# Two heads of 16 dimensions in two row tiles: scores and maxima of the narrow attention, in steps of two key chunks

## The reference

```python
# x: normalized queries; keys, values: the context
q, k, v = split_heads(x @ Wq), split_heads(ctx @ Wk), split_heads(ctx @ Wv)   # 16 heads of 16
scores = einsum('bhqd,bhkd->bhqk', q, k) / sqrt(16)
scores = where(arange(4096) < valid_lens[b], scores, -1000000.0)
out = einsum('bhqk,bhkd->bhqd', softmax(scores), v) @ Wo
```

## Time and profile before

| | us |
|---|---|
| median of 3 runs | 4371.15 (4368.67 to 4373.83) |
| the profiled execution: its own time | 4371.64 |
| its span, from first to last instruction | 4369.9 |
| narrow attention's cycles, 2732 to 3775 | 1043 |
| in the whole span: TensorE busy | 3948.9 (90%) |
| VectorE busy | 2704.8 (62%) |
| ScalarE busy | 2369.3 (54%) |

### The profile page before, as it was taken

How to read it: one execution, slowest core, us unless ns; L and a number is a source line. 1 busy time by engine, 2 the same in 40 slices (tenths; PEclk the granted TensorE clock), 3 DMA queues, 4 the chain that set the end, 5 groups by cost and what they waited for, 6 DMA issues and landing times. The chain is left out here.

```text
span 4369.9 us, 74948 instructions
## 1 busy us (share of the span) xinstructions
PE 3948.9 (90%) x26760; PEld 2746.4 (63%) x26760; DVE 2704.8 (62%) x4112; ACT 2369.3 (54%) x4373; POOL 1552.2 (36%) x1229
## 2 busy tenths in 40 slices
PE   5899999999999999998677976999999999676599
PEld 2677777777777777776446965555555555343365
DVE  4766666666666666663264124677776777476666
ACT  2677777777777777776142112555555566444111
POOL 1566666666666666666022003000000000033000
PEclk9999999999999999999788987999999999888799
DMA  5777767777677666662203647544444422100011
GB/s 194 273 252 252 248 241 260 256 256 250 239 265 252 247 232 222 232 224 80 78 10 121 266 171 261 151 156 137 142 148 141 120 58 65 31 2 5 18 37 42
DMA packets 232703, 724.77 MB, mean 166 GB/s; under 512 B 44557, under 2 KB 129805, under 8 KB 163725
## 3 DMA queue, kind: packets, MB, share of 16 engines
q1 hardware_dynamic: 229664, 711.78, 47.8%
q0 software_dynamic: 2688, 8.39, 0.5%
HBM read 625.70 MB, written 94.37 MB: 165 GB/s over the span
## 5 line engine op out<-in xcount | busy, mean ns | idle before, releaser
L752 POOL TENSOR_TENSOR wa_acc<-wa_acc,wa_probs 128x512 f32<-128x512 f32 x960 | 1246.5, 1298 | 525.1 <-ACT wa_probs L613 444.9
L677 DVE TENSOR_REDUCE wa_mx<-wa_ps_m 128x2 f32<-128x1024 f32 x512 | 626.6, 1224 | 486.1 <-PE wa_ps_m L488 485.9
L613 ACT ACTIVATE wa_probs<-wa_ps_s 128x512 f32<-128x512 f32 x1024 | 556.3, 595 | 525.5 <-PE wa_ps_s L534 520.2
L1204 ACT ACTIVATE na_probs<-na_ps_s 128x512 f32<-128x512 f32 x1024 | 564.1, 599 | 377.8 <-PE na_ps_s L1108 372.4
L1256 DVE TENSOR_REDUCE na_mx<-na_ps_m 128x1 f32<-128x512 f32 x1024 | 643.0, 681 | 186.8 <-PE na_ps_m L1093 185.8
L605 ACT ACTIVATE wa_ps_s<-wa_m_wide 128x512 f32<-128x512 f32 x1024 | 575.7, 605 | 1.0
L510 PE MATMUL wa_ps_o<-wa_probs,wa_values 128*64 128x256 f32 x4096 | 505.3, 389 | 0.0
L1093 PE MATMUL na_ps_m<-na_keys,na_q 98*128 98x512 f32 x1024 | 425.8, 424 | 41.7 <-DVE na_mx L1256 28.6
L1108 PE MATMUL na_ps_s<-na_q,na_keys 100*128 100x512 f32 x1024 | 429.8, 427 | 2.4 <-ACT na_probs L1204 1.6
L449 PE MATMUL wa_ps_k<-wa_k_ctx,wa_w_k 128*128 128x512 f32 x1488 | 388.6, 396 | 0.0
L475 PE MATMUL wa_ps_v<-wa_w_v,wa_v_ctx 128*128 128x256 f32 x2880 | 382.5, 282 | 0.0
(11 more groups left out here) (329 smaller groups left out, 5108.6 us busy)
## 6 DMA issues: line engine op xcount, KB each, us to landing
wa_k_ctx<-ctx_split SPq DMA_DIRECT2D x248, 1024.0 KB, 5.1
wa_v_ctx<-ctx_split SPq DMA_DIRECT2D x120, 1024.0 KB, 5.7
na_ctx<-ctx_split SPq DMA_DIRECT2D x56, 1024.0 KB, 6.9
na_keys<-k_rows SPq DMA_DIRECT2D x192, 256.0 KB
ctx_split<-wa_stage SPq DMA_DIRECT2D x32, 1024.0 KB, 9.7
wa_land<-in_ctxT SPq DMA_DIRECT2D x32, 512.0 KB, 10.3
ge_w_b<-in_w_rows SPq DMA_DIRECT2D x8, 2048.0 KB
k_rows<-na_k_high SPq DMA_DIRECT2D x64, 256.0 KB, 2.3
```

The lines of the kernel that those rows point to most:

```text
L613: act.activation(probs[:, c % R:c % R + 2, h * SQ:(h + 1) * SQ], ps_s[n % BANKS][:, :].rearrange("p (c n) -> p c n", c=2), ACT.Exp).then_i ...
L677: dve.tensor_reduce(mx[:, half, :, k], ps_m[:, :, :], AX.X, ALU.max).then_inc(m_taken, 1)
L752: pool.tensor_tensor(acc[:, :], acc[:, :], probs[:, c % R, :], ALU.add).then_inc(summed, 1)
L1204: act.activation(probs[:, n % RP, :], ps_s[n % RS][:, :], ACT.Exp).then_inc(exp_done, 1)
```

## The change

Each head of the pair gets a row tile of its own: its four mask and shift rows and 48 key rows lie at rows 0 to 51 for the first head and 64 to 115 for the second. `q` loses the second block and its zeros.

- Scores come in steps (`t`, 16 a cycle) of two chunks: four products of 52 rows x 256 columns, two for each head. A bank of `ps_s` now holds one head's scores for two chunks. There are still three banks, and a step begins when the exponentials of all but the last bank are done (n+2-3).
- Maxima come in units (`u`, 16 a cycle): the same 128 queries of both heads, two products of 52 rows x 512 columns into two banks. The rows of the shift, which the maxima must not see, are cleared by GpSimd (`clear_shift`, two small instructions a cycle).
- The order of a cycle's work changes: the last weighting of a cycle goes into the next cycle's step 1, `turn_maximum` goes ahead of the second half of the values' projection, `copy_out` from the cycle's start to step 2, `divide` to step 4. The shift is copied by two instructions.
- The keys of one half are loaded by 8 transfers, where there were 4.

```diff
     DH = 16
     W = 2 * DH
-    MASK = 3 * W
-    MROWS, ROWS = MASK + 2, MASK + 4
+    HEAD = 64
+    KEYS = 4
+    ROWS = KEYS + 3 * DH
+    ST = CH // 2
     VW = DH + 1
...
-        q = [s.sb(f"q{i}", [P, 2, SQ], F32R) for i in range(3)]
+        q = [s.sb(f"q{i}", [P, SQ], F32R) for i in range(3)]
...
-        def steps(c):
-            return (2 * c, 2 * c + 1) if c < 3 else (c + 3,) if c + 3 < CH else ()
+        def units(t):
+            return (2 * t, 2 * t + 1) if t < 2 else (t + 2,) if t + 2 < ST else ()
...
-                for t in range(3):
-                    rows = (2 * b + t % 2) * D + i * W
-                    sp.dma_start(keys[a % 2][t * W:(t + 1) * W, cols].bitcast(F32), k_rows[rows:rows + W, cols]
+                sp.wait_ge(edge_stored, 1 + 16 * (b + 1))
+                for h in range(2):
+                    r = h * HEAD
+                    sp.dma_start(keys[a % 2][r:r + KEYS, cols].bitcast(F32), edges[4 * b:4 * b + 4, cols]
                                  ).then_inc(keys_in[a % 2][half], 16)
-                sp.wait_ge(edge_stored, 1 + 16 * (b + 1))
-                sp.dma_start(keys[a % 2][MASK:ROWS, cols].bitcast(F32), edges[4 * b:4 * b + 4, cols]
-                             ).then_inc(keys_in[a % 2][half], 16)
+                    for t in range(3):
+                        rows = (2 * b + t % 2) * D + i * W + h * DH
+                        sp.dma_start(keys[a % 2][r + KEYS + t * DH:r + KEYS + (t + 1) * DH, cols].bitcast(F32),
+                                     k_rows[rows:rows + DH, cols]).then_inc(keys_in[a % 2][half], 16)
...
-            def maximum(a, i):
-                u, j = divmod(i, 4)
-                n = a * CH + i
-                if i == 0:
+            def maximum(a, u):
+                k, half = divmod(u, 2)
+                if u == 0:
                     pe.wait_ge(q_in[a % 3], 1 + 96 * (a // 3 + 1))
-                if i in (0, CH // 2):
-                    pe.wait_ge(keys_in[a % 2][2 * i // CH], 1 + 64 * (a // 2 + 1))
-                if i == 2:
-                    pe.wait_ge(q_ready, 1 + a)
-                pe.wait_ge(m_taken, 1 + max(n + 1 - RM, 0))
-                pe.matmul(ps_m[n % RM][:, :], q[a % 3][0:MROWS, j // 2, (j % 2) * P:(j % 2 + 1) * P],
-                          keys[a % 2][0:MROWS, u * 512:(u + 1) * 512], start=True, stop=True).then_inc(m_done, 1)
+                    pe.wait_ge(q_zero, 1 + 2 * (a + 1))
+                if u in (0, ST // 2):
+                    pe.wait_ge(keys_in[a % 2][2 * u // ST], 1 + 128 * (a // 2 + 1))
+                for h in range(2):
+                    n = a * CH + 2 * u + h
+                    if u == 1 and h == 0:
+                        pe.wait_ge(q_ready, 1 + 2 * a)
+                    pe.wait_ge(m_taken, 1 + max(n + 1 - RM, 0))
+                    r = slice(h * HEAD, h * HEAD + ROWS)
+                    pe.matmul(ps_m[n % RM][:, :], q[a % 3][r, half * P:(half + 1) * P], keys[a % 2][r, k * 512:(k + 1) * 512],
+                              start=True, stop=True).then_inc(m_done, 1)
             def turn_maximum(a):
                 pe.wait_ge(msplit_ready, 1 + a + 1)
                 for j in range(4):
-                    ins = pe.matmul(ps_m[((a + 1) * CH + 2) % RM][MASK:ROWS, j * P:(j + 1) * P], msplit[:, j, :].bitcast(F32),
-                                    ident[:, :], start=True, stop=True)
+                    h, half = divmod(j, 2)
+                    ins = pe.matmul(ps_m[((a + 1) * CH + 2) % RM][h * HEAD:h * HEAD + 2, half * P:(half + 1) * P],
+                                    msplit[:, j, :].bitcast(F32), ident[:, :], start=True, stop=True)
                 ins.then_inc(mT_done, 1)
-            def scores(a, c):
-                n = a * CH + c
-                if c == 0:
-                    pe.wait_ge(q_ready, 1 + a + 1)
-                pe.wait_ge(exp_done, 1 + max(n + 1 - RS, 0))
-                pe.matmul(ps_s[n % RS][:, :], keys[a % 2][0:ROWS, c * P:(c + 1) * P],
-                          q[a % 3][0:ROWS, :, :].rearrange("p h n -> p (h n)"), start=True, stop=True).then_inc(s_ready, 1)
+            def scores(a, t):
+                n = a * CH + 2 * t
+                if t == 0:
+                    pe.wait_ge(q_ready, 1 + 2 * (a + 1))
+                pe.wait_ge(exp_done, 1 + max(n + 2 - RS, 0))
+                for i in range(2):
+                    for h in range(2):
+                        r = slice(h * HEAD, h * HEAD + ROWS)
+                        ins = pe.matmul(ps_s[(n + h) % RS][:, i * SQ:(i + 1) * SQ], keys[a % 2][r, (2 * t + i) * P:(2 * t + i + 1) * P],
+                                        q[a % 3][r, :], start=True, stop=True)
+                        if i:
+                            ins.then_inc(s_ready, 1)
...
-                for c in range(CH):
-                    scores(a, c)
+                for t in range(ST):
+                    scores(a, t)
                     if a + 1 < G:
-                        for i in steps(c):
-                            maximum(a + 1, i)
-                    if c == 3 and a:
+                        for u in units(t):
+                            maximum(a + 1, u)
+                    if t == 3 and a:
                         pe.wait_ge(masked, 1 + 2 * min(a + FIRST, N))
                         pe.wait_ge(v_ready, 1 + 2 * min(a + CG, N))
                         add_up(a - 1)
-                    if c == 12 and kb is not None:
+                    if t == 1 and a:
+                        weigh(a - 1, CG - 1)
+                    elif t % 2 and t > 1:
+                        weigh(a, t // 2 - 1)
+                    if t == 7 and kb is not None:
                         pe.wait_ge(o_ready, 1 + a)
                         project_keys(kb, 0, ps_p)
-                    if c == 18 and kb is not None:
+                    if t == 10 and kb is not None:
                         pe.wait_ge(masked, 1 + 2 * kb + 1)
                         project_keys(kb, 1, ps_p)
-                    if c == 24 and vb is not None:
+                    if t == 13 and vb is not None:
                         pe.wait_ge(o_ready, 1 + a)
                         pe.wait_ge(masked, 1 + 2 * min(a + FIRST + 1, N))
                         project_values(vb, 0, ps_p)
-                    if c % 4 == 1 and c > 4:
-                        weigh(a, c // 4 - 1)
+                if a + 1 < G:
+                    turn_maximum(a + 1)
                 if vb is not None:
                     pe.wait_ge(v_ready, 1 + 2 * vb + 1)
                     project_values(vb, 1, ps_p)
-                if a + 1 < G:
-                    turn_maximum(a + 1)
-                weigh(a, CG - 1)
+            weigh(G - 1, CG - 1)
...
-            def exponents(a, c):
-                n = a * CH + c
-                act.wait_ge(s_ready, 1 + n + 1)
-                if n >= RP:
-                    act.wait_ge(pv_done, 1 + (n - RP) // 4 + 1)
-                act.activation(probs[:, n % RP, :], ps_s[n % RS][:, :], ACT.Exp).then_inc(exp_done, 1)
+            def exponents(a, t, h):
+                c = a * CH + 2 * t
+                act.wait_ge(s_ready, 1 + c + h + 1)
+                if c >= RP:
+                    act.wait_ge(pv_done, 1 + (c - RP) // 4 + 1)
+                act.activation(probs[:, c % RP:c % RP + 2, h * SQ:(h + 1) * SQ],
+                               ps_s[(c + h) % RS][:, :].rearrange("p (c n) -> p c n", c=2), ACT.Exp).then_inc(exp_done, 1)
             def take_maximum(a):
                 act.wait_ge(mT_done, 1 + a + 1)
-                act.activation(q[a % 3][MASK:ROWS, :, :].rearrange("p h n -> p (h n)"), ps_m[((a + 1) * CH + 2) % RM][MASK:ROWS, :],
-                               ACT.Copy).then_inc(q_ready, 1)
+                for h in range(2):
+                    act.activation(q[a % 3][h * HEAD:h * HEAD + 2, :], ps_m[((a + 1) * CH + 2) % RM][h * HEAD:h * HEAD + 2, 0:SQ],
+                                   ACT.Copy).then_inc(q_ready, 1)
...
-                for c in range(CH):
-                    exponents(a, c)
-                    if c == 16 and kb is not None:
+                for t in range(ST):
+                    for h in range(2):
+                        exponents(a, t, h)
+                    if t == 9 and kb is not None:
                         take_high(kb, 0)
-                    if c == 22 and kb is not None:
+                    if t == 12 and kb is not None:
                         take_high(kb, 1)
-                    if c == 28 and vb is not None:
+                    if t == 14 and vb is not None:
                         take_values(vb, 0, ps_p)
...
-                if a:
-                    copy_out(a - 1)
-                for c in range(CH):
+                for t in range(ST):
+                    if t == 2 and a:
+                        copy_out(a - 1)
                     if a + 1 < G:
-                        for i in steps(c):
-                            take_maximum(a + 1, i)
-                    if c == 6 and a:
```

(14 more changed lines are left out.)

60 lines of the change are left out of this document (33 added, 27 removed).

## The result

The kernel after takes **4528.69 us** (median of 4 runs, 4510.77 to 4533.77), the kernel before 4371.54 in the same comparison (4368.67 to 4373.83). The ratio is 1.035, with a 95% interval of 1.033 to 1.038: slower by 157 us where 17 were forecast. The profiled execution took 4528.14 us, its span 4526.4.

The account below looks back on a forecast made before the run. TensorE was taken to set the pace; the cycles' chain of waits summed to 20 x 0.73 + 3 x 0.11 + 7 x 0.36 = +17.4 us, so 4388.5 us. Its own range was 4375 to 4403, for 8 in 10 4364 to 4410.

Parts of the forecast that it names:

- the chain: Sequence of waits and products through a cycle's 16 steps: 35.01 us in cycles 1 to 20, where it was 34.28.
- S1: Start of step 1's scores: 1.86 us after the cycle's first scores.
- S7: Start of step 7's scores, after the wait behind `divide`: 14.24 us after the cycle's first scores.
- The end: End of each of cycles 1 to 20, after half the values' projection: 35.01 us.
- the turned maxima: Near a cycle's end, after the last weighting: at 32.4 us, 0.77 for them, then values of 1.4 to 1.6.
- no change: Rival: the same chain with small errors, 0.4 to 0.8 us a cycle less, 4366 to 4379 us; chance 0.17.
- pairs overlap: Two row tiles run at once: a step's scores 0.24 us, a unit's maxima 0.23; rival without overlap 4506, chance 0.03.
- weight loads stay under cover: A score step's four weight loads stay hidden; the rival with them bare gave 4438 us, chance 0.04.
- bank waits bind: Steps wait for the previous step's first exponential: score groups at least 1.19 us apart, even steps stall 0.62.
- a rival at 0.10: Bank wait does not bind: five stalls' 3.3 us go, a cycle takes 32.4, the kernel some 4315 us; chance 0.10.
- TensorE's time: TensorE's busy time down by 5 us a cycle or more, with the cycle no shorter.
- the clock falls: Rival: TensorE waits more and runs at 1.2 GHz; four such cycles give 4448 us; chance 0.02.

Follow-up runs that it names:

- run 3: The changed kernel with each head's scores waiting for their own bank instead of one wait ahead of all four products: 4503.37 us.
- run 5: The changed kernel with extra products that nothing reads put where TensorE waits, no wait shortened: 4418.39 us.
- run 10: The kernel before with score and maximum products over rows 0 to 63 only, same columns, order and waits, mask and shift left out: 4587.42 us.

## Why the prediction was wrong

- **Right: the chain; the direction by luck.** A full-clock cycle was forecast at 35.01 and took 34.57; every step's start stands within 0.35 us of the forecast. S1 came 0.34 early and S7 0.33: behind a unit's second product the next scores were put 0.34 later, but they are the other head's, in the other row tile, and start with it (both at 1.52). The end came 0.44 early, 0.23 of it at the turned maxima, 0.54 apart from the values where 0.77 stood. The other 0.21 is in no term of the forecast: turned maxima at 32.4, 0.77 and values of at most 1.6 make 34.8, not 35.01, and the values took 1.63. By the chain alone the kernel would stand at +8 us, 4379, the edge of "no change". So the forecast "slower" came out right for a reason that it did not have: of the 157 us the chain has 8.
- **Right: pairs overlap, weight loads stay under cover, bank waits bind** (1.19 from even to odd steps). That the stalls could be had back was a rival at 0.10, and run 3 shows why they can't with three banks of two chunks: the wait moves to the second head. (The 32.4 us a cycle of that rival do not follow from its 3.3: 35.01 less 3.3 is 31.7.)
- **Partly right: TensorE's time.** 29.98 busy a cycle for 33.44: 3.5 less, not 5, and as forecast the cycle is no shorter for it.
- **Wrong: the rival "the clock falls", at a chance of 0.02.** The step that failed is "in the last cycle four chunks take 2.66, of which the products' distances fill 4 x 0.23 + 0.99 = 1.9, and the clock stays at 2.4 GHz". It compared how much of the time is filled and took a column for a column, while the last cycle's products have 100 rows and the changed ones 52. The row was of the other layout and couldn't carry the claim: after the change the same last cycle runs at 1.2 GHz for some 20 of its 28.1 us. What the runs showed in its place: 344 us of the stage at 1.2 GHz, 129 of the 157 us, of which filled waits give 110 back (run 5), and a clock that over 64 rows falls even with the waits as they were (run 10). Its price was off as well: it took four fallen cycles at 15 us each, and it was nearly every cycle, at some 4 us.
- **The range.** 4364 to 4410 left this case out, and the time lies 119 us above it.

The Trainium skill, in TensorE: Matmul & The Clock Gate, section HAM oscillation — how this bites in real kernels, puts such falls down to gaps in which TensorE idles. Run 5 agrees in part (84 us at 1.2 GHz where there were 344); run 10 doesn't, with TensorE 95% busy ahead of the fall and 460 us at 1.2 GHz. The measurement decides. The Trainium skill's "Up to 2×" of TensorEngine Tiling (Array Packing), section Theoretical Speedup, was real for the pairs: two products within 0.39 us, the length of one.

## What to carry to other kernels

Before packing operands of few rows into row tiles, look for a row of the same layout, with nothing but such products around it, and read its granted clock; in this case a row of products over 100 rows was no evidence. A saving on the engine that sets the pace is worth only what the next waits leave: here 3.5 us a cycle of TensorE's time became none. Work that can move into a wait is worth more than work that is made cheaper: moving one weighting and two smaller pieces gave 27 us, without a new layout.

## What was not expected of the hardware

- With the same columns and waits and TensorE busy 97% to 98% of the stage, the time at 1.2 GHz was 12 us over 98 and 100 rows, 207 over 66, 460 over 64 (the last two without mask and shift).
- With half the columns over the full rows it was 61 us, none in cycles 1 to 20.
- Useless products of 64 rows, put into waits, gave back 110 us of a kernel of 4529. Why the clock falls with fewer rows, and whether a row tile counts apart from its rows, stays open.
